# A differential-attention block on one core: ScalarE scales units 0 and 6 of each eight instead of units 2 and 6

## What is computed

```
x = x + attention(layernorm(x));  x = x + ffn(layernorm(x))
# in attention:
attn_w = softmax(q @ k^T)                            # 16 of them, in 8 pairs
attn_w = attn_w[:, :, 0] - lam * attn_w[:, :, 1]     # one head from each pair
attn   = attn_w @ v;  attn = gamma * attn / (rms(attn) + eps) * (1 - LAMBDA_INIT)
return attn @ Wout
# ffn: a gated causal attention over 16 experts
```

## Time and profile before

| | |
|---|---|
| median of 3 runs | 1399.73 us (1397.35 to 1400.1) |
| the profiled execution | 1397.11 us, of which the traced span is 1394.9 us |
| first attention, with its pipeline filling and draining | about 37 to 1045 us of the span |
| one half-step, where all is steady | 30.54 us |

### The profile page before, as it was taken

One profiled execution on the slowest core, in us unless ns is written; L12 is line 12 of the kernel. 1 busy time (PEld: TensorE's weight loads), 2 busy tenths in 40 slices (PEclk: granted clock), 3 DMA queues, 4 the chain that ended last, 5 costly groups with the idle time before them and its releaser, 6 DMA issues. The chain is left out here.

```text
span 1394.9 us, 24022 instructions
## 1 busy us (share of the span) xinstructions
PE 1219.2 (87%) x8370; PEld 748.1 (54%) x8370; DVE 1187.9 (85%) x1937; ACT 1101.6 (79%) x2031; POOL 1027.0 (74%) x714
## 2 busy tenths in 40 slices
PE   2789999999999999999999999998862599999997
PEld 1344444444444444444444444444431498989897
DVE  5899999999999999999999999999858576767674
ACT  3899999999999999999999999999833455656553
POOL 3788898899989889998988999899942744434320
PEclk9899999999999999999999999999975799999999
DMA  4232111121211112121111212110003876768570
GB/s 112 70 89 63 48 37 51 31 56 44 62 47 39 52 31 55 42 66 42 42 52 31 55 41 65 35 31 1 1 6 55 151 130 120 137 112 146 100 130 10
DMA packets 184598, 86.85 MB, mean 62 GB/s; under 512 B 150176, under 2 KB 166048, under 8 KB 184480
## 3 DMA queue, kind: packets, MB, share of 16 engines
q1 hardware_dynamic: 184480, 85.33, 28.8%
HBM read 7.68 MB, written 2.10 MB: 7 GB/s over the span
## 5 line engine op out<-in xcount | busy, mean ns | idle before, releaser
L1246 DVE TENSOR_REDUCE negmax<-score_ps 128x1 f32<-128x1024 f32 x512 | 617.8, 1217 | 47.8 <-PE score_ps L609 45.8
L490 POOL TENSOR_TENSOR prob<-prob 128x1024 f32<-128x1024 f32 x256 | 603.6, 2358 | 50.4 <-ACT prob L966 34.4
L925 ACT ACTIVATE prob<-score_ps,negmax 128x1024 f32<-128x1024 f32 x512 | 571.1, 1118 | 61.5 <-DVE negmax L1246 60.7
L609 PE MATMUL score_ps<-ka,qa 128*128 128x512 f16 x1024 | 307.9, 383 | 83.5 <-ACT prob L925 72.1
L638 PE MATMUL attn_ps<-probT,v_sb 128*64 128x512 f32 x1024 | 276.0, 619 | 0.8 <-ACT attn_nT L973 0.8
L632 PE MATMUL trans_ps<-ident,prob 128*128 128x128 f32 x2048 | 269.3, 274 | 0.8 <-POOL prob L490 0.3
L632 PEld LDWEIGHTS trans_ps<-ident,prob 128*128 128x128 f32 x2048 | 238.4, 141 | 56.2 <-issue 2.0
L557 POOL TENSOR_TENSOR xs<-xnT,rw_all 128x2048 f32<-128x2048 f32 x32 | 117.4, 3671 | 147.3 <-DVE prob L1379 140.5
L488 POOL TENSOR_SCALAR prob<-prob,ccol 128x1024 f32<-128x1024 f32 x192 | 215.2, 1121 | 3.3 <-DVE ccol L1259 3.3
L609 PEld LDWEIGHTS score_ps<-ka,qa 128*128 128x128 f16 x1024 | 80.5, 97 | 218.5 <-ACT prob L925 151.9
L332 DVE COPY probT<-trans_ps 128x512 f32<-128x512 f32 x256 | 174.1, 680 | 1.8 <-PE trans_ps L632 1.8
(11 more groups left out here) (195 smaller groups left out, 1321.5 us busy)
## 6 DMA issues: line engine op xcount, KB each, us to landing
qa<-split SPq DMA_DIRECT2D x256, 64.0 KB, 2.0
ka<-split SPq DMA_DIRECT2D x256, 64.0 KB, 2.0
xg<-xnT SPq DMA_DIRECT2D x16, 512.0 KB, 3.0
resid<-in_L_attn_x SPq DMA_DIRECT2D x4, 512.0 KB, 6.3
wg<-in_L_attn_Wkv SPq DMA_DIRECT2D x32, 64.0 KB, 2.0
out<-prob SPq DMA_DIRECT2D x32, 64.0 KB, 2.6
wg<-in_L_attn_Wq SPq DMA_DIRECT2D x16, 64.0 KB, 1.9
xsT<-prob SPq DMA_TRANSPOSE x64, 4.5
```

The lines of the kernel that those rows point to most:

```text
L490: pool.tensor_tensor(prob1[:, n % PROBS, :], prob1[:, n % PROBS, :], prob2[:, n % 4, :], ALU.add).then_inc(mix_ok, 1)
L609: mm = pe.matmul(score_ps[:, sub, kh * HALF:(kh + 1) * HALF], qa[:, par, head * 2 + sub, q0:q0 + P], ka[:, par, head * 2 + sub, kh * HALF: ...
L925: act.activation(prob2[:, n % 4, :] if sub else prob1[:, n % PROBS, :], score_ps[:, sub, :], ACT.Exp, bias=negmax[:, s % 2, sub:sub + 1], ...
L1246: dve.tensor_reduce(negmax[:, s % 2, sub:sub + 1], score_ps[:, sub, :], AX.X, ALU.max, negate=True).then_inc(max_ok, 1)
```

## The change

The units whose second probabilities ACT scales are now 0 and 6 of each eight; unit 2 goes to POOL. ACT still makes 64 such scalings and POOL 192.

```
-ACT_SCALES = (2, 6)
+ACT_SCALES = (0, 6)
```

## The result

The median went from 1399.49 us (20 runs, 1397.35 to 1400.1) to 1402.24 us (20 runs, 1398.84 to 1403.87). The ratio is 1.0019, with a 95% interval of 1.0013 to 1.0026: 1.8 to 3.6 us more. 1402.6 us was predicted, with +2.9 us for the change. The profiled execution of the changed kernel took 1402.47 us, of which its span is 1400.3 us.

A forecast was written before the change was run, and what follows sets the result against it. A chain of waits through DVE, PE and ACT, not any engine's sum of work, was taken to set the half-step. At +0.10 us for 29 half-steps, +2.9 us on 1399.73 gave 1402.6 us, range 1398.8 to 1406.

The forecast's parts named there:

- Slot 3, what is removed: Unit 2's scaling leaves ACT ahead of exp (4,0); at most 0.72 us a half-step can be had at score (5,0).
- Slot 1, what is added: Unit 0's scaling now stands on ACT between exp (1,1) and exp (2,0), making score (3,0) 0.82 us late.
- What that lateness does: PE's 6.37 us from score (3,0) to score (4,1) cannot shrink, so all of slot 3 moves by about 0.8 us.
- Exp (4,0): On ACT in slot 4: starts at 629.61, hardly earlier than 629.66; it allows score (5,0) at 630.96, PE comes at 631.11.
- The tight part: From score (5,0) to exp (1,1), 19.58 us: DVE runs through except for 0.3 us, so lateness stays.
- POOL: Its add of unit 0 waits for ACT; unit 2 is done at 631.76, over 5 us before PE needs it: no cost.
- The rival that it falls behind at the end: POOL's add of unit 0 waits, costing 0.5 us at the end of the attention: 1403.1 us; chance 0.04.
- The extra waits at score (5,0): Score (5,0) on PE might cost 0.11 us more through its several waits: 0.20 us a half-step, 1405.5 us; chance 0.20.
- The sum: Seven terms from one score (5,0) to the next make a half-step of 30.64 us against 30.54, +0.10 us.
- slower: Outcome for the whole kernel's time, with 0.2% or 2.8 us as the line from no change; chance 0.48.
- same: Outcome of no change in the whole kernel's time, within about 0.2% or 2.8 us; chance 0.44.
- The advice to look for the gaps and make what blocks there start sooner: By it, closing slot 4's gap with nothing replacing it gains 20.9 us: 1378.8 us, the faster rival; chance 0.08.

The follow-up runs named there:

- second profile of the kernel before: The kernel before, unchanged, run and profiled once more at the end of the experiments; 1399.19 us, steady half-step 30.54 us.
- the removal: Against the kernel before, ACT scales only unit 6 and nobody scales unit 2, nothing added in slot 1; 1375.37 us, ratio 0.9829.
- the addition: Against the kernel before, unit 2 stays on ACT and unit 0 comes to it, so ACT scales units 0, 2 and 6; 1424.03 us, ratio 1.0184.
- first profile of before: The kernel before, unchanged, in the profiled execution that the prediction was read from; 1397.11 us.

## Why the prediction was right

*Slot 3, what is removed.* Right: 0.71 us with that half alone, 0.72 predicted. The transposes at 634.11 and score (5,0) at 634.98 lie 0.87 us apart, without a wait.

*Slot 1, what is added.* Right: 0.83 us with that half alone, 0.82 predicted. The terms are 625.01 - 623.91 = 1.10, 626.06 - 625.01 = 1.05 and 627.30 - 626.06 = 1.24 us, where 1.11, 1.04 and 1.24 had been read elsewhere in the half-step.

*What that lateness does.* Right: from score (3,0) to score (4,1) it takes 633.68 - 627.30 = 6.38 us (6.37), so nothing is caught up. The tight part is 623.91 - 604.33 = 19.58 us, as before.

*Exp (4,0).* Right: it starts 633.46 - 604.33 = 29.13 us after the last score (5,0), where it was 629.66 - 600.47 = 29.19; PE comes later and decides.

*POOL.* Right: the add of unit 2 starts at 602.65 and is done 2.37 us later, and PE transposes that unit at 610.59 (slot 6), 5.6 us after. With a seventh scaling the steady half-step still didn't suffer. The rival that it falls behind at the end did not come true here (the last spacing but one is 24.35 us, 24.20 in the second profile of the kernel before), but the mechanism is real: it cost 3.5 us with unit 0 a slot later, and 2.4 us with seven scalings.

*The extra waits at score (5,0)*, the cost that the trace did not settle, are not paid: 0.87 us. (Written out, 29 x 0.11 would be 3.2 us, where the prediction had 2.9.) The longer way of 1.35 us is seen only where the score waits for an exponential. The Trainium skill, in Perfetto Trace Analysis under Identifying Dependency Chains, allows for extra semaphore instructions ahead of an instruction that waits on several engines; no row shows whether any stand here. The 0.87 us say that nothing is paid where the others are done before PE is.

*The sum.* 19.58 + 1.10 + 1.05 + 1.24 + 6.38 + 0.43 + 0.87 = 30.65 us, 30.64 predicted. The 0.01 us is within the rounding that was stated; in all, 3.4 us by the exact quotients, 2.9 predicted, 1.8 to 3.6 measured. The ratio of 1.0019 lies on the line of 0.2%, and its interval on both sides of it, so these runs don't decide between the prediction's "slower" and "same". That 1402.6 and 1402.24 lie within 0.4 us is in part luck: the median of the three runs that the sum started from was 0.24 us above that of all twenty. Nothing was taken for the first two half-steps, and that held for the change as a whole: its first copy of slot 3 starts at 111.92 us, that of the second profile of before at 111.97. For the halves alone it did not hold: 110.39 us with the removal, 114.12 with the addition.

*The profiled time* is what the prediction had no term for: 1400.0 was worked out from the profiled execution, and 1402.47 came. About 1.9 of those 2.5 us are not the change's: the first copy of slot 3 starts at 111.92 us where it was at 109.99. Some 0.4 more are the half-step, 0.116 us longer instead of 0.10. The first profile of before was of an execution in which the clock rose early; the 2.6 us by which it lay under the median, which the sum took over without a cause, are about the 2.1 us by which it lies under the second profile. Working from the difference and not from the span was what kept the forecast right.

*The advice to look for the gaps and make what blocks there start sooner* (the Trainium skill, Perfetto Trace Analysis, Optimization Strategy) led to a gap that is worth closing: closing it alone is worth 0.71 us a half-step. But the time follows only if the work is put where no earlier link of the same chain waits for it. The changed kernel closes the gap and loses 2.75 us; with unit 1 in place of unit 0 it is closed too, and the time is 1384.33 us, where the kernel before took 1399.15 on that chip.

## What to carry to other kernels

Moving a short piece of work between idle places of an engine that is not full changes no sum, so ask at both places which instruction behind it starts a chain without slack; three neighbouring places for one scaling of 1.04 us cost 0.83, 0.51 and 0.23 us a half-step (30.66, 30.34 and 30.06 less 29.83). Cost the removal and the addition each by itself, from the start of the last instruction whose time is fixed to the next; then they add up. And before a sum of a few us is set against a profile, look at the granted clock in that one execution.

## What the hardware showed that was not expected

The granted clock of TensorE came back at different times in different executions of the same kernel. At the start of the attention PE waits some 10 us for a transfer, and the clock falls in that wait; the timeline of the changed kernel:

```profile
35.35 1.89 PE L609 MATMUL score_ps<-ka,qa 128*128 128x512 f16 x4 [9.89 <-DMA ka<-split]
```

Windows of 5 us (busy time of each engine, then the granted clock, DMA share, GB/s), first of the changed kernel, then of the kernel before, its second profile and its first:

```profile
25.00:30.00 5.00, 0.46 (x5) 0.27 (x3) 4.13 (x11) 3.84 (x6) 0.56 (x1) 1.00 0.45 105
30.00:35.00 5.00, 0.00 (x0) 0.00 (x0) 2.04 (x7) 0.45 (x2) 2.13 (x2) 0.50 0.46 107
...
40.00:45.00 5.00, 4.15 (x14) 1.81 (x12) 4.15 (x7) 3.73 (x7) 0.00 (x0) 0.50 0.45 104
45.00:50.00 5.00, 3.02 (x9) 1.23 (x8) 3.85 (x6) 4.20 (x9) 4.62 (x3) 0.50 0.53 211
50.00:55.00 5.00, 4.95 (x23) 3.89 (x24) 3.17 (x5) 3.97 (x8) 4.92 (x4) 0.61 0.00 2
```

```profile
45.00:50.00 5.00, 3.21 (x10) 1.24 (x10) 4.09 (x6) 4.30 (x8) 3.76 (x3) 0.50 0.53 211
50.00:55.00 5.00, 5.00 (x23) 3.98 (x22) 2.95 (x6) 4.87 (x9) 2.49 (x2) 0.62 0.00 2
```

```profile
40.00:45.00 5.00, 3.12 (x13) 1.04 (x11) 4.49 (x8) 3.78 (x6) 3.51 (x3) 0.79 0.44 102
45.00:50.00 5.00, 3.12 (x18) 1.74 (x18) 4.32 (x6) 4.71 (x10) 3.39 (x2) 1.00 0.53 210
```

1.00 is the upper level, 2.4 GHz, and 0.50 the lower, 1.2 GHz; a number between them is the mean of a window. Two executions of one kernel differ by some 10 us in when the upper level is back, and their first copies of slot 3 by 111.97 - 109.99 = 2.0 us; the late rise belongs to no kernel. Of the 2.0 us, 0.3 lie ahead of the first exponential already (37.70 against 37.37), and 1.65 are added while the clocks differ, up to exp (5,0) of the first half-step (56.26 against 54.28).

At the end of the attention, where PE stands 2.51 us for POOL, the clock fell early in some profiles and later in others. The output projection after it, in the timeline of the changed kernel, and in that with unit 0 ahead of exp (1,1):

```profile
1034.55 2.08 PE L692 MATMUL misc_ps<-wo_sb,attn_nT 128*128 128x128 f32 x8
```

```profile
1025.08 1.16 PE L692 MATMUL misc_ps<-wo_sb,attn_nT 128*128 128x128 f32 x8
```

The order and the waits of this stretch are the same in both, the 2.51 us included; the clock is 0.85 and then 0.81 in the windows 1030:1035 and 1035:1040 of the first, and 1.00 from 1021 to 1026 in the second. The last spacing is 14.71 us in the first and 13.14 in the second: 1.6 us for the lower clock. The rows account for all of it: the projection takes 2.08 us against 1.16, the products (L638) ahead of it 1.58 against 1.08 and those behind it 1.23 against 1.08. These two are different kernels, and both profiles of the kernel before have the long spacing (14.71 and 14.76 us), so whether the kernel or the execution decides here is not shown. That these two places make the spread of the timed runs (before 1397.35 to 1400.1) fits their sizes. The mean granted clock of the changed kernel's twenty runs points the same way: 0.973 in the fastest (1398.84 us), 0.970 or 0.971 around the median, 0.968 in the slowest (1403.87 us). But timed runs have no rows, so the two places are argued and not shown. Why the clock comes back sooner in one execution than in another stays open.
